# W2 two steps further behind W1, and a new order of the steps of a pair

## The reference

```python
h = jnp.concatenate([tokens(x), txt], axis=1)                 # 64 x 193 x 128
h = h + attention(layernorm(h))                               # 8 heads, relative positions, two group norms
h = h + ffn(layernorm(h))
# ffn: probs = softmax(x @ Wg); top_p = top 2 of 8, normalized
#      for i in range(2):   # every expert, both times
#          g = gelu(einsum('btd,edf->ebtf', x * top_p[..., i:i+1], W1) + b1)
#          out = out + einsum('ebtf,efd->btd', g, W2) + sum(b2)
```

## Time and profile before

| | |
|---|---|
| time, median of 2 runs | 2931.16 us (2927.7 to 2934.63) |
| time of the profiled execution | 2932.71 us |
| its span, first to last instruction | 2930.8 us |
| mean granted TensorE clock | 0.994 of full speed |
| PE busy, share of the span | 2862.8 us, 98% |
| PE weight loads busy | 2294.8 us, 78% |
| DVE busy | 1975.8 us, 67% |
| ACT busy | 1957.8 us, 67% |
| POOL busy | 1025.8 us, 35% |
| chain of waits that ended last: PE, ACT, DVE, DMA | 83%, 7%, 4%, 2% |

### The profile page before, as it was taken

How to read it: one execution, slowest core, us unless ns; L and a number is a source line. 1 busy time by engine, 2 the same in 40 slices (tenths; PEclk the granted TensorE clock), 3 DMA queues, 4 the chain that set the end, 5 groups by cost and what they waited for, 6 DMA issues and landing times.

```text
span 2930.8 us, 65392 instructions
## 1 busy us (share of the span) xinstructions
PE 2862.8 (98%) x21348; PEld 2294.8 (78%) x21348; DVE 1975.8 (67%) x4885; ACT 1957.8 (67%) x4640; POOL 1025.8 (35%) x999
## 2 busy tenths in 40 slices
PE   6998899999999999999999999999999999999998
PEld 6996777777777778777777777777777787777776
DVE  4665666776676667666666666666766676666665
ACT  4564467776766667766666677766666677666666
POOL 0000233434333434434333334444333344343334
PEclk9999999999999999999999999999999999999999
DMA  9994011111111011111110111111110111111100
GB/s 184 213 207 137 17 31 36 31 36 36 34 33 32 15 36 31 36 36 36 31 36 19 28 36 31 36 36 36 31 34 13 36 31 36 36 36 31 33 9 12
DMA packets 104390, 134.79 MB, mean 46 GB/s; under 512 B 10110, under 2 KB 98750, under 8 KB 99902
## 3 DMA queue, kind: packets, MB, share of 16 engines
q1 hardware_dynamic: 97442, 131.00, 19.8%
q10 hardware_dynamic: 6896, 3.09, 0.5%
HBM read 118.97 MB, written 15.07 MB: 46 GB/s over the span
## 4 chain that ended last, share of the span: by engine, by line
PE 83%; ACT 7%; DVE 4%; issue 3%; DMA 2%; SPq 1%; POOL 0%; DVEq 0%; ACTq 0%; POOLq 0%
PE bank L398 20%; PE bank L407 7%; PE bank L499 6%; PE bank L553 6%; PE bank L552 6%; PE bank L520 6%; PE bank L408 6%; PE bank L411 6%; PE bank L585 4%; ACT arena L949 4%; PE bank L506 4%; PE bank L534 3%; PE bank L562 2%; DVE mx L745 1%; SPq L339 1%
## 5 line engine op out<-in xcount | busy, mean ns | idle before, releaser
L1014 POOL TENSOR_TENSOR arena<-arena 128x386 f32<-128x386 f32 x672 | 734.5, 1100 | 710.4 <-ACT arena L893 702.5
L892 ACT ACTIVATE arena<-bank,b_s 128x386 f32<-128x386 f32 x1024 | 596.0, 582 | 445.5 <-DVE arena L614 396.0
L398 PE MATMUL bank<-arena,w_s 128*128 128x386 f32 x2048 | 831.2, 490 | 0.3 <-POOL arena L1014 0.2
L614 DVE TENSOR_TENSOR arena<-bank,ratio 128x386 f32<-128x386 f32 x1024 | 571.2, 559 | 269.0 <-PE bank L411 247.4
L893 ACT ACTIVATE arena<-arena,b_s 128x386 f32<-128x386 f32 x1024 | 623.2, 609 | 0.0
L407 PE MATMUL bank<-x_hi,w_hi 128*128 128x386 f32 x1024 | 577.2, 564 | 2.5 <-ACT x_hi L965 1.8
L949 ACT ACTIVATE arena<-bank,mx 128x193 f32<-128x193 f32 x800 | 325.9, 425 | 163.9 <-DVE mx L745 163.9
L398 PEld LDWEIGHTS bank<-arena,w_s 128*128 128x128 f32 x2048 | 369.1, 190 | 20.9 <-POOL arena L1014 10.6
L408 PE MATMUL bank<-x_hi,w_lo 128*128 128x386 f32 x1024 | 350.2, 342 | 0.0
L411 PE MATMUL bank<-x_lo,w_hi 128*128 128x386 f32 x1024 | 348.8, 341 | 0.0
L499 PE MATMUL bank<-rw,arena 128*128 128x193 f32 x1600 | 318.5, 339 | 4.1 <-DVE arena L735 3.9
(11 more groups left out here) (155 smaller groups left out, 4215.1 us busy)
## 6 DMA issues: line engine op xcount, KB each, us to landing
a_rep<-u_scratch SPq DMA_DIRECT2D x32, 1600.0 KB, 9.8
arena<-in_x SPq DMA_DIRECT2D x192, 196.0 KB
g_bc<-g_scratch SPq DMA_DIRECT2D x64, 193.0 KB, 3.6
hk<-in_txt SPq DMA_DIRECT2D x32, 128.0 KB, 2.5
u_scratch<-k_f SPq DMA_DIRECT2D x32, 100.0 KB, 2.2
u_scratch<-q_f SPq DMA_DIRECT2D x32, 100.0 KB, 2.2
out<-o_s SPq DMA_DIRECT2D x64, 48.5 KB
out<-o_s SPq DMA_DIRECT2D x64, 48.0 KB
```

The costliest lines, as they stand in the source:

```text
L398: mm(yb[:, 0:T2], w2_s[:, f, :], gelu1[:, f % RING, :], start=(f == 0), stop=(f == NF - 1)).then_inc(S["w2_done"], 1)
L614: v.tensor_tensor(gelu2[:, f % RING, :], zb[f % 2][:, 0:T2], ratio[:, :], ALU.mult).then_inc(S["z2_done"], 1)
L892: a(gelu1[:, f % RING, :], zb[f % 2][:, 0:T2], ACT.Gelu, bias=b1_s[:, f:f + 1]).then_inc(S["g_done"], 1)
L1014: g.tensor_tensor(gelu1[:, f % RING, :], gelu1[:, f % RING, :], gelu2[:, f % RING, :], ALU.add).then_inc(S["pool_sum"], 1)
```

## The change

`LAG` goes from 4 to 6, and the list is put in another order. With LAG 6, the W2 matmul of step f-6 stands in step f; steps 4 and 5 have none any more, and the last six W2 steps (26 to 31) of a pair are `~w2t` in the next turn.

```diff
-LAG = 4
+LAG = 6
 SCHEDULE = (
-    "qs0 ~grow ~w2t vt ~w2t am0 log0 am1 ~w2t qs1 log1 ~w2t qs2 am2 log2 qs3 log3 ~ot am3 log4 log5 ~hres ~bcast log6 log7 qs4 ~xin hkeep log8 log9 log10 ~otr log11 log12 txt tr0 ~a st1 tr1 ~a rel0 ~a tr2 rel1 nb1 tr3 inv rel2 tr4 rel3 tr5 rel4 ~ocopy tr6 xt1 rel5 ~a c rel6 proj pv0 rec0 gmean c pv1 rec1 gvar place0 place1 C gaff c omean c c C C nqk ovar C c C C oaff onorm C oh2 c swap mean2 C var2 nv top C c gate C C c c c c c c c gate2 c c"
+    "vt am0 qs0 ~grow ~w2t ~w2t log0 ~w2t am1 ~w2t ~w2t ~w2t log1 am2 log2 qs1 log3 ~ot am3 log4 log5 qs2 log6 log7 ~hres ~bcast ~xin hkeep log8 qs3 qs4 log9 ~otr log10 log11 log12 txt tr0 ~a tr1 st1 ~a rel0 ~a tr2 ~a ~ocopy inv nb1 rel1 tr3 c rel2 tr4 rel3 tr5 rel4 xt1 tr6 rel5 rel6 proj pv0 gmean c gvar pv1 rec0 rec1 place0 place1 C gaff c omean c C C nqk ovar C c C C oaff onorm C c C oh2 c C mean2 swap c C var2 top c c c gate C c c c C nv gate2 c c"
 ).split()
```

More of the change, by code:

```diff
@@ L90 @@
 SCHEDULE = (
-    "qs0 ~grow ~w2t vt ~w2t am0 log0 am1 ~w2t qs1 log1 ~w2t qs2 am2 log2 qs3 log3 ~ot am3 log4 log5 ~hres ~bcast log6 log7 qs4 ~xin hkeep log8 log9 log10 ~otr log11 log12 txt tr0 ~a st1 tr1 ~a rel0 ~a tr2 rel1 nb1 tr3 inv rel2 tr4 rel3 tr5 rel4 ~ocopy tr6 xt1 rel5 ~a c rel6 proj pv0 rec0 gmean c pv1 rec1 gvar place0 place1 C gaff c omean c c C C nqk ovar C c C C oaff onorm C oh2 c swap mean2 C var2 nv top C c gate C C c c c c c c c gate2 c c"
+    "vt am0 qs0 ~grow ~w2t ~w2t log0 ~w2t am1 ~w2t ~w2t ~w2t log1 am2 log2 qs1 log3 ~ot am3 log4 log5 qs2 log6 log7 ~hres ~bcast ~xin hkeep log8 qs3 qs4 log9 ~otr log10 log11 log12 txt tr0 ~a tr1 st1 ~a rel0 ~a tr2 ~a ~ocopy inv nb1 rel1 tr3 c rel2 tr4 rel3 tr5 rel4 xt1 tr6 rel5 rel6 proj pv0 gmean c gvar pv1 rec0 rec1 place0 place1 C gaff c omean c C C nqk ovar C c C C oaff onorm C c C oh2 c C mean2 swap c C var2 top c C c gate C c c c C nv gate2 c c"
 ).split()
```

## The result

The changed kernel takes 3085.60 us (median of 2 runs, 3085.14 to 3086.05), 1.0523 times the kernel before (95% interval 1.0488 to 1.0557). It is 154 us slower, where the forecast was 2 us.

A forecast was written before the change was run, and what follows sets the result against it. PE sets the pace, busy 82.67 of 83 us a turn. Gains of 22.8 us against losses of 25.1 gave +2.3 on the median of 2931.16; forecast 2933 us, range 2910 to 2950.

The forecast's parts named there:

- the edits that cost nothing: Moves and added work on DVE, ACT, POOL and SP, such as a twelfth DVE sum of 0.55 us, priced at zero.
- ACT's debt: Rival: GELUs late at `onorm`, again at `swap` and `nv`, hold W1 and the seam: 2990 us and more; 4%.
- The rival at the seam: POOL's sum holds up DVE's `am0`; `log0` some 0.5 to 0.7 us late each turn, up to 2953 us; 20%.
- mean2: PE's L426 waits 0.28 us for DVE's residual, plus 0.11 for late weights; both go: gain 0.39 us a turn.
- var2: PE's `var2` starts 0.22 us late, waiting for DVE's square; two steps now cover it: gain 0.22 us a turn.
- am1: PE's wait at L499 for L735, 3.9 us over the span, should go: two more W2 matmuls stand before it.
- onorm: On ACT, now before GELU 15, so W1 of step 17 waits: loss 0.48 us a turn, bounds 0.18 to 0.48.
- gvar: Only one W1 stands between `gmean` and `gvar`, so PE waits for DVE: loss 0.34 us on 30 turns, possibly nothing.

The follow-up runs named there:

- after_pad40: The changed kernel with 40 one-column memsets on DVE just ahead of the first turn, outside the loop: 2940.22 us, ratio 1.0014 to the kernel before.
- after_pad40_sums: after_pad40 with DVE doing the sums of steps 16, 18 and 20 instead of 15, 17 and 19: 2915.09 us.
- lag6_only: The kernel before with LAG 6 alone, two more `~w2t` between `am1` and `qs1`, nothing else moved: 2925.70 us, ratio 0.9969.
- after_terms_rec: after_terms with `rec0` put back behind `pv0` and `rec1` behind `pv1`, both ahead of `gvar`: 2904.45 us.
- after_terms: after_pad40_sums with `gvar` put back behind `pv1` and `otr` behind `log10`: 2923.51 us.
- before_pad40: The kernel before with 40 one-column memsets on DVE ahead of the first turn: 2927.72 us, ratio 0.9965.

## Why the prediction was wrong, point by point

**The step that failed.** The sum was one of waits between engines, and "the change gives PE the same instructions in another order", so that it "can only win waits, and it can only lose by new ones". That left out a cost which no order of the list shows: the fetching of the instructions themselves. The added sum on DVE was put among the edits that cost nothing, because it "falls where DVE idles". It was counted as one and is two (steps 23 and 29 make it thirteen sums against eleven), and their 0.55 us of work each do fall there. But they and one other instruction make DVE's loop three instructions longer, two more instructions ahead move it, and that set off 28 stalls of 3.4 us at the one place where DVE's next operation is awaited by PE. With the lower clock behind them that is 145 of the 154 us. The page of before has a line on it, 18 packets of instructions for a program that runs its loop 29 times: nothing was fetched anew in a pass. How near that was to changing I did not ask. The chance of 4% for "slower by over 2%" was worked out from ACT's debt alone; what I had not seen got 3%.

**The place was nearly right.** The rival at the seam had `am0` late and L499 waiting for L735, and named the line that the trace now shows, with the wrong cause. In after_pad40 DVE is first: it is done with the sum of step 29 and starts `am0` some 0.2 us after `grow`; POOL's sum starts at 0.39 and is the one that is held, 1.71 us long. PE starts `log0` at 1.41, in time. That rival did not come.

**`mean2`.** The wait of 0.28 went, as forecast. Of the 0.39 only 0.13 came in, because W1 of step 20 waited 0.26 for a GELU that was late through `oh2`. I had DVE need "some 0.8 for `oh2`", by the row of before, and did not ask what POOL does at that time. In after_pad40_sums all of it comes in (W1 to W1 over `mean2` in 1.82 us instead of 2.22).

**`var2`.** Forecast 0.22, measured 0.32 over the same interval (W1 to W1 from 2.89 to 2.57 us). The size was off, the mechanism right. But W1 of step 24 lost 0.57, for which the forecast has no term.

**`am1`.** The size was right by luck. The 3.9 us of the earlier trace rows are four waits ahead of the loop, in turns without an old pair's W2 behind them, and lag6_only still has 3.8 of them. What the two W2 matmuls cover is another lateness of `am1`, 0.23 us in 15 of the turns, which the line does not count; the 31 turns together are 3.9 us shorter, and that the two figures are the same is chance.

**`onorm`.** Right within 0.03 us: W1 of step 17 came 1.63 to 1.65 us after step 16's in the changed kernel, 0.45 to 0.47 late, forecast 0.48. With ACT's queue in that place:

```profile
1595.42 0.98 ACT L962 ACTIVATE t<-t,gst_o 128x193 f32<-128x193 f32 x2
1596.30 0.56 ACT L892 ACTIVATE arena<-bank,b_s 128x386 f32<-128x386 f32 x1
```

```profile
1595.57 0.34 PE L408 MATMUL bank<-x_hi,w_lo 128*128 128x386 f32 x1
...
1597.20 0.34 PE L408 MATMUL bank<-x_hi,w_lo 128*128 128x386 f32 x1
```

**`gvar`.** Forecast 0.34, measured 0.24 at `gvar` itself. The time from `gmean` to `gvar` is 1.10 us where 0.86 are needed:

```profile
1578.00 0.39 PE L480 MATMUL bank<-mv,con 128*128 128x4 f32 x2
...
1579.10 0.39 PE L483 MATMUL bank<-gst,con 128*128 128x4 f32 x2
```

The 0.11 of late weights did not come; they were carried over from `mean2`, whose matmul has 386 columns, to one with 4. And of the 0.24 only 0.11 is left at the next W1, as after_terms_rec shows.

**Costed at nothing.** `swap`, `nv`, `vt`, the transposes and masks, `hres` and `bcast` cost nothing, as said. `otr` ahead of `log10` was not named at all: it costs 0.20 us (after_terms and after_terms_rec have it back). The likely reason, by the order of the queues, is that it holds up the maxima and exponentials of `log10`, and `tr0` waits for the last of these.

**The sum without the stall.** By parts of the turn, after_pad40 less before, the W2 matmuls taken out at 0.65 each, means of 25 turns: from W1 of step 31 to W1 of step 0 -0.12 us, from there to step 6 +0.11, to step 17 +0.44, to step 31 +0.05; together +0.47, for a turn of 83.46 against 83.00. Forecast was +0.07. Waits of 0.83 us behind meetings with POOL were not seen. Against them stand 0.2 more of gains in the same part of the turn (after_pad40_sums gains 0.81 there, counted were 0.61) and 0.2 less of loss at `gvar`. `otr`'s 0.20 is in the first part, and something of the same size that I did not count made up for it there.

So without the fetch the forecast of 2933 would have met 2940, inside its range. That would have been luck in part: errors that cancel in the turn, and an embedding stage that was 7 us shorter in the profile of after_pad40 than in that of before. Against before_pad40 the order costs 12.5 us, where 2.3 were forecast.

## What to carry to other kernels

When a change makes a loop's program on any engine longer, or moves it, compare the packets of the instruction queues and the idle time with the releaser "issue" at the first instruction of a pass: an edit of a few instructions turned a stall of 3.4 us on in every pass, and dummy instructions ahead of the loop turned it off. Count the instructions in the kernel that is run: one sum more stood in it than I had counted. Before you believe in an order written for several engines, lay DVE's operations on two SBUF inputs beside POOL's timeline; which engine takes which sum was worth 0.83 us a turn, more than all that the new order was forecast to win. And when you move a name, look at what stands behind it on each engine's queue: `rec0` behind `gvar` made PE wait 0.55 us a turn, more than the two moves had won.

## What the runs showed of the hardware

- A branch back on DVE took 0.27 us where the loop's body lay in three blocks of 128 instructions, and 2.76 to 3.70 us where it lay in four, with five packets of 8192 B fetched in each pass. A loop with one block too many is fetched anew in every pass. Within a place the stall is nearly constant: 2.76 to 3.06 in both kernels that are 128 instructions apart, 3.43 to 3.70 in the changed kernel.
- What a stall of 3.4 us costs is more than 3.4 us. PE stood for 3.18 us and then had the lower clock (0.50) for some 3.4 us, 1.69 us more for the same matmuls. Where it stood for 2.13 us, three turns of the loop had this and 25 had not.
- DVE's operations with two SBUF inputs that begin beside a sum of POOL end 0.01 to 0.42 us after it: `oh2`'s first addition took 1.17 us instead of 0.37, the square 1.20 instead of 0.56. A sum of POOL that begins 0.13 us behind such an operation can hold it too: 1.16 us for a subtraction of 97x4, which takes 0.17 otherwise. POOL's reciprocal root of 97x4 did not hold the same subtraction, in any turn of after_pad40_sums. The forecast knew this rule for the seam and applied it there only.
